# A one-core transformer block: the second batch's attention in two sweeps, with its last projection and routing inside the loop

## What is computed

```
x = x + 0.5 * ffn(layernorm(x))        # first mixture-of-experts layer
x = x + attention(layernorm(x))        # 16 heads, latent width 64, causal
x = x + 0.5 * ffn(layernorm(x))        # second one, same weights
```

```
pos  = cumsum(onehot(expert of each choice)) - 1
keep = pos < 320
out_e = (silu(buf @ wg) * (buf @ wu)) @ wd       # buf: the tokens scattered by (expert, pos)
routed[token] += gate * keep * out_e[expert, pos]
```

## Time and profile before

| | |
|---|---|
| median of 3 runs | 1077.17 us |
| the profiled execution | 1078.49 us, of which its span is 1076.7 us |
| PE busy | 873.8 us, 81% of the span |
| DVE, ACT, POOL busy | 567.6, 406.9, 399.4 us |
| chain that ended last | PE 52%, DVE 15%, POOL 10%, SP queue 7%, DMA 7%, issue 7% |
| mean granted TensorE clock | 0.94 |

### The profile page before, as it was taken

How to read it: one execution, slowest core, us unless ns; L and a number is a source line. 1 busy time by engine, 2 the same in 40 slices (tenths; PEclk the granted TensorE clock), 3 DMA queues, 4 the chain that set the end, 5 groups by cost and what they waited for, 6 DMA issues and landing times.

```text
span 1076.7 us, 16412 instructions
## 1 busy us (share of the span) xinstructions
PE 873.8 (81%) x5041; PEld 720.3 (67%) x5041; DVE 567.6 (53%) x1624; ACT 406.9 (38%) x803; POOL 399.4 (37%) x583
## 2 busy tenths in 40 slices
PE   2358599992678998998999799899999845899993
PEld 1235477771246887987888488888888823687773
DVE  6743245444369665665752575566641362345444
ACT  2101132321314564554641454656566211233323
POOL 2677266654002222221210111354642046356651
PEclk9999699997789999999999899999999868899997
DMA  9510345553620011114101001112110100446536
GB/s 357 205 49 25 104 145 177 172 153 118 196 53 1 20 43 30 43 41 139 30 21 42 1 10 34 42 51 60 47 34 21 40 21 25 146 138 190 167 105 198
DMA packets 96245, 94.11 MB, mean 87 GB/s; under 512 B 15274, under 2 KB 83004, under 8 KB 95415
## 3 DMA queue, kind: packets, MB, share of 16 engines
q1 hardware_dynamic: 86966, 81.00, 25.1%
q0 software_dynamic: 9216, 12.33, 3.7%
HBM read 54.95 MB, written 37.03 MB: 85 GB/s over the span
## 4 chain that ended last, share of the span: by engine, by line
PE 52%; DVE 15%; POOL 10%; SPq 7%; DMA 7%; issue 7%; ACT 1%; POOLq 0%; DVEq 0%; ACTq 0%
PE PS L1375 15%; PE PS L1282 8%; POOL xbuf L552 7%; PE PS L1269 6%; SPq L499 6%; PE PS L1331 5%; PE PS L1270 5%; PE PS L1356 4%; PE PS L1406 3%; DVE mxp L1052 3%; DVE den L1096 2%; DMA rden<-den 2%; DVE xs L1034 2%; PE PS L1243 2%; POOL area_o L588 2%
## 5 line engine op out<-in xcount | busy, mean ns | idle before, releaser
L1375 PE MATMUL PS<-pT,area_v 128*128 128x256 f32 (+1 forms) x1280 | 307.7, 364 | 20.4 <-POOL pT L568 20.2
L1052 DVE TENSOR_REDUCE mxp<-PS 128x2 f32<-128x512 f32 (+1 forms) x320 | 197.7, 630 | 149.5 <-PE PS L1331 81.9
L752 ACT ACTIVATE pT<-PS 128x512 f32<-128x512 f32 (+1 forms) x320 | 176.7, 554 | 186.7 <-PE PS L1356 183.9
L1375 PEld LDWEIGHTS PS<-pT,area_v 128*128 128x128 f32 x1280 | 211.7, 192 | 36.8 <-issue 22.5
L602 POOL DMA_INDIRECT ybuf<-area_o,yidx x160 | 155.6, 973 | 128.5 <-DVE area_o L1008 89.5
L1331 PE MATMUL PS<-Kz,Qx 128*128 128x256 f32 (+1 forms) x640 | 169.0, 355 | 17.5 <-DVE mxp L1052 11.1
L552 POOL DMA_INDIRECT xbuf<-xn,sidx x128 | 125.4, 980 | 88.3 <-issue 62.0
L1356 PE MATMUL PS<-Qx,Kz 128*128 128x256 f32 (+1 forms) x640 | 142.7, 305 | 6.6 <-ACT pT L752 5.5
L1331 PEld LDWEIGHTS PS<-Kz,Qx 128*128 128x128 f32 x640 | 113.6, 196 | 39.0 <-DVE mxp L1052 19.6
L588 POOL TENSOR_TENSOR area_o<-area_o,rden 128x512 f32<-128x512 f32 x32 | 40.7, 1271 | 258.5 <-DMA rden<-den 258.5
L568 POOL TENSOR_SCALAR_AFFINE_SELECT pT<-pT 128x128 f32<-128x128 f32 x256 | 67.7, 299 | 178.9 <-ACT pT L752 178.6
(11 more groups left out here) (160 smaller groups left out, 859.2 us busy)
## 6 DMA issues: line engine op xcount, KB each, us to landing
area_v<-xbuf SPq DMA_DIRECT2D x32, 340.0 KB, 3.2
area_v<-in_L_ffn_wg_dram SPq DMA_DIRECT2D x32, 256.0 KB, 3.4
area_v<-in_L_ffn_wu_dram SPq DMA_DIRECT2D x32, 256.0 KB, 3.7
area_v<-in_L_ffn_wd_dram SPq DMA_DIRECT2D x64, 128.0 KB, 2.5
rden<-den SPq DMA_DIRECT2D x256, 32.0 KB, 1.8
yg<-ybuf SPq DMA_DIRECT2D x24, 256.0 KB, 4.3
qkbuf<-stage SPq DMA_DIRECT2D x24, 256.0 KB, 3.0
xbuf<-Kz SPq DMA_DIRECT2D x4, 1360.0 KB, 10.9
```

The costliest lines, as they stand in the source:

```text
L752: nc.scalar.activation(pT[:, N % 4, 0:w], PS[:, 2 + N % 2, 0:w], ACT.Exp).then_inc(exp_done, 1)
L1052: nc.vector.tensor_reduce(mxp[:, i, c, 2 * hp:2 * hp + 2], PS[:, k % 2, 0:2 * w].rearrange("p (h w) -> p h w", h=2), AX.X, ALU.max).then_i ...
L1375: ins = mm(PS[:, pv_bank(U, a), (p + 1) * TC - w:(p + 1) * TC], value_and_ones(j, h), pT[:, N % 4, a * w:(a + 1) * w], start=(first and p ...
```

## The change

- Steps are numbered over both batches in *visits* (batch, group, chunks). Batch 0 has 4 visits of all four chunks, as before. Batch 1 has 4 visits of chunks 0 to 2 (24 steps each), then 4 visits of chunk 3 (16 steps each), so 12 visits and 12 loads of q and k in place of 8 and 8. A load is 5 DMAs (q of 4 heads in one, k of each head in one; 32 rows a head), not 8. The constant rows of `qkbuf` are written at the start.
- New row items in batch 1's chunk-3 steps: "O" is `out_proj` and residual of one tile (tiles 0 to 5, at steps 272 to 282), "Y" the LN transposes, "S" the scores, "C" the counts of those six tiles. LN statistics, routing (route 4, six tiles) and the Sqrt and Exp tables for them stand between steps 286 and 310; 12 of the 24 scatters of the six tiles stand at steps 313 to 324.
- Tiles 6 and 7 (route 5) follow after the loop, mixed with the shared network (`last_part`). `sil` and `hb` move to the area of the values.
- Row items: 18 ahead of the loop, 186 in batch 0's steps, 169 in batch 1's. Each visit's last T stands right after its last R; before, three items later.
- Start: x arrives as the first DMA, LN and scores of batch 0 are done in halves; one of POOL's two 128x4096 memsets goes behind the first 64 scatters.
- Into attention: combine, LN, J, stores and loads of visit 0 in two halves of 512 tokens; the maxima of chunks 0 and 1 need the first half alone.

Core of the diff (the splitting of `ln`, `shared` and `ln_std_dev` into parts is left out):

```diff
+VISITS = [(0, g, tuple(range(NCH))) for g in range(NG)] + [(1, g, c) for c in (tuple(range(NCH - 1)), (NCH - 1,)) for g in range(NG)]
+STEPS = [(v, c, j, p) for v, (b, g, chunks) in enumerate(VISITS) for c in chunks for j in range(2 * c + 1, -1, -1) for p in range(2)]
+O_STEPS = [FIRST[V_LAST - 2] + 2 * i for i in range(HT - 2)]
+S_STAT, S_ROWS, S_TURN, S_SCORE = FIRST[V_LAST - 1] - 2, FIRST[V_LAST - 1], FIRST[V_LAST - 1] + 1, FIRST[V_LAST] - 1
+S_GROUP, S_EXP, S_HOT, S_GATE, S_COUNT = [FIRST[V_LAST] + k for k in (1, 3, 4, 4, 6)]
+SCAT_LAST = [n for n in range(S_COUNT + 3, len(STEPS) + 5)]
...
+EXTRA = [(O_STEPS[i], ("O", i)) for i in range(HT - 2)] + [(S_TURN, ("Y", 0, 3)), (S_TURN + 1, ("Y", 3, 6)), (S_SCORE, ("S", 4)),
+         (S_COUNT, ("C", 4)), (TAIL, ("O", 6)), (TAIL, ("O", 7)), (TAIL, ("Y", 6, 8)), (TAIL, ("S", 5)), (TAIL, ("C", 5))]
...
+def row_steps():
+    steps, end = [-1] * N_EARLY, 0
+    for v, visit in enumerate(VISITS):
+        mine = [k for k, (vk, item) in enumerate(PLAIN) if vk == v and k >= N_EARLY]
+        last = max(UNIT_FIRST[U] for U, (vu, c) in enumerate(UNITS) if vu == v) - 2
+        begin = 0 if v == 0 else max(end, FIRST[v - 1] + 3)
+        steps += [begin + i * (last - begin) // len(mine) for i in range(len(mine))]
+        end = last
...
-ROUTES = [(0, 0, HT // 2), (0, HT // 2, HT), (1, 0, HT), (0, 0, HT), (1, 0, HT // 2), (1, HT // 2, HT)]
+ROUTES = [(0, 0, HT // 2), (0, HT // 2, HT), (1, 0, HT), (0, 0, HT), (1, 0, HT - 2), (1, HT - 2, HT)]
...
+            def visit_in(v, cols, arrived):
+                b, g, chunks = VISITS[v]
+                heads = qkbuf[b, :, HG * g:HG * g + HG, :, cols]
+                sp.dma_start(Qx[v % 2][:, cols].bitcast(F32), heads[0].rearrange("h r t -> (h r) t")).then_inc(arrived, 16)
                 for hh in range(HG):
+                    sp.dma_start(Kz[v % 2][RW * hh:RW * hh + RW, hh, cols].bitcast(F32), heads[1, hh]).then_inc(arrived, 16)
...
+                if step in FIRST[1:-1]:
+                    v = FIRST.index(step) + 1
+                    sp.wait_ge(st_ready, step)
+                    visit_in(v, slice(0, T), qk_in[v % 2])
-            sp.wait_ge(wo_x, 2 * HT)
+            sp.wait_ge(pv_done, len(STEPS))
             expert_pairs(1)
...
+            def last_part():                     # TensorE
+                pe.wait_ge(exp_done, len(STEPS))
+                pe.wait_ge(y_free, 2 * len(UNITS))
+                gate_up_rows(1, 0)
+                for k in LAST_ROWS[0:2]:
+                    row_item(k)
+                gate_up_rows(1, 1)
+                down_rows(1, 0)
+                for k in LAST_ROWS[2:4]:
+                    row_item(k)
+                gate_up_rows(1, 2)
+                down_rows(1, 1)
+                row_item(LAST_ROWS[4])
+                gate_up_rows(1, 3)
+                down_rows(1, 2)
+                down_rows(1, 3)
...
+            def last_part():                     # VectorE
+                hidden_rows(1, 0)
+                for k in LAST_ROWS[0:2]:
+                    row_item(k)
+                last_stats(1)
+                ln_rows(5, 1, 1, *LN_LAST[1])
+                hidden_rows(1, 1)
+                shared_x(1, 0)
+                for k in LAST_ROWS[2:4]:
+                    row_item(k)
+                for step in (route_groups, route_experts, route_hot):
+                    step(5)
+                hidden_rows(1, 2)
+                shared_x(1, 1)
+                row_item(LAST_ROWS[4])
```

More of the change, by code:

```diff
@@ L60 @@
 RW = 32
-R0 = 2
-RQ = R0 + 3 * HD
+R0 = RW - 3 * HD
 VP = 3 * LAT
@@ L70 @@
 C_TOK, C_EID, C_K, C_N = 560, 576, 581, 585
[L73 to L118, removed]
-def rows_at(step):
-    return [k for k, s in enumerate(ROW_STEP) if s == step]
[L125 to L132, removed]
-LAST = [(0, 1), (1, 3), (3, 6), (6, 8)]
-LAST_PE = 6
-ROUTES = [(0, 0, HT // 2), (0, HT // 2, HT), (1, 0, HT), (0, 0, HT), (1, 0, HT // 2), (1, HT // 2, HT)]
+ROUTES = [(0, 0, HT // 2), (0, HT // 2, HT), (1, 0, HT), (0, 0, HT), (1, 0, HT - 2), (1, HT - 2, HT)]
 L1 = 3
@@ new lines, with rows_at @@
+ROWS = sorted([(step, 0, k, *PLAIN[k]) for k, step in enumerate(row_steps())] +
+              [(step, 1, k, V_LAST, item) for k, (step, item) in enumerate(EXTRA)])
+ROW_STEP = [row[0] for row in ROWS]
+ROW_ITEMS = [row[3:] for row in ROWS]
+ROW_NUMBER = {item if item[0] != "R" else (v, item): k for k, (v, item) in enumerate(ROW_ITEMS)}
+LAST_ROWS = [k for k, step in enumerate(ROW_STEP) if step == TAIL]
+def rows_at(step):
+    return [k for k, s in enumerate(ROW_STEP) if s == step]
+EVAC, RECIP, SCALE_AT, DRAIN = LAG + 1, LAG + 5, LAG + 10, 16
@@ L151, in pv_bank, with units_at @@
+def units_at(step, delay, b):
+    return [U for U, s in enumerate(UNIT_STEP) if s + delay == step and VISITS[UNITS[U][0]][0] == b]
+LAST = [(0, 1), (1, 3), (3, 6), (6, 8)]
+LAST_PE = 6
 def pv_bank(U, a):
@@ L1228, in shared, with down_rows @@
-                down(3)
+                for q in range(4):
+                    gate_up_rows(L, q)
+                    if q:
+                        down_rows(L, q - 1)
+                down_rows(L, 3)
+            def down_rows(L, q):
+                pe.wait_ge(sh_h, 8 * L + 2 * q + 2)
+                if q >= 2:
+                    pe.wait_ge(sh_x, 4 * L + q - 1)
+                for c in range(HC):
+                    for t in range(4):
+                        ins = mm(PS[:, 6 + q % 2, t * D:(t + 1) * D], hb[q % 2][:, c, t * P:(t + 1) * P], sdw[:, c, :],
+                                 start=(c == 0 and t == 0), stop=(c == HC - 1), skip_group_check=True)
+                ins.then_inc(sh_y, 1)
@@ L1413, in _ @@
             pe.wait_ge(s_ctc, 1)
-            ln(0, 0)
-            for f in range(2):
-                scores(f, 0)
+            scores(0, 0)
+            ln_half(0, 0, 1)
+            scores(1, 0)
+            pe.wait_ge(s_cst, 1)
             for f in range(2):
```

693 lines of the change are left out of this document (409 added, 284 removed).

## The result

| | us |
|---|---|
| before, median of 4 runs | 1076.56 (1074.43 to 1077.93) |
| after, median of 4 runs | 1090.56 (1081.44 to 1092.05) |
| ratio | 1.011, interval [1.008, 1.014] |
| forecast | 1049 (1033 to 1064) |

What follows compares the result with a forecast made beforehand. TensorE was taken to bound the attention loops, and chains of waits over other engines the stages between. The terms -5.1 - 27.7 + 1 + 33.5 - 29.8 gave -28.1 us, so 1049 us, range 1033 to 1064.

Steps and rivals of the forecast that it cites:

- Start (-5.1): Before POOL's first scatter: LN and scores in halves save DVE's waits for ACT and scores, 5.1 us, ends 2 and 7.
- Into attention (-27.7): Way to the first attention step: row scores start earlier and fewer items stand ahead of the loop, 27.7 us saved.
- Batch 0's steps (+1): Batch 0's attention loop: three more items and T waits cost, batch 1's combines among fewer items save; 1 us longer.
- The J in group 2 stay as they are: Batch 0's loop: batch 1's q and k projections keep their place, so no cost was added.
- Batch 1's steps (+33.5): Batch 1's attention loop: moved-in row items, O, LN, scores, counts, T waits and loads make it 33.5 us longer.
- The load term, 1.0: Chunk-3 visits of batch 1: waits for q and k loads cost 1.0 us in all, ends 0 and 18.
- The argument against late loads: Chunk-3 sweep: SP has no spreading where loads stand, against the 9% rival of loads waited for in full (1071 us).
- no change, ends -5 and +8: Batch 1's loop: `pv` waits for masks behind `scale` on in-order POOL stay as before, with these ends in us.
- The end (-29.8): Last `pv` to the second expert layer's first transpose: 53.1 us in place of 82.9, with 3.8 for a lower clock.
- The rival of the cold tail: After the loop: TensorE's work stays at 1.2 GHz, some 10 us more, 1059 us; 16%.
- holes filled: Batch 1's loop: new items fall into TensorE's idle time, 14 of 18.6 us go, 1035 us; 14%.
- The rival of a cold sweep: Batch 1's second sweep: waits keep the clock at 1.2 GHz, slower than before; half of it cold gives 1102 us; 4%.

Runs made afterwards that it cites:

- runs 5 and 6: POOL's `scale` put behind later masked steps, in the changed kernel (1056.5 us, ratio 0.980) and in the kernel before (1055.17 us, 0.979).
- run 2: Changed kernel with batch 1's four J in two pairs, at steps 108, 109, 114 and 115: 1081.24 us, ratio 1.002.
- run 1: Changed kernel with the last T of each visit two steps behind its last R: 1082.27 us, ratio 1.005.
- all three edits: Changed kernel with last T two steps later, batch 1's J in two pairs and `scale` behind the masks: 1040.61 us, ratio 0.965.
- run 8: Changed kernel with the T, J and `scale` edits together: 1040.61 us, ratio 0.965 to the kernel before.
- runs 1 to 4: Changed kernel with T moved; J paired; last tiles' items behind the loop; the same with one sweep: 1082.27, 1081.24, 1120.42, 1098.81 us.
- `scale` edit: A unit's `scale` on POOL put behind masked steps of a later unit; in the kernel before: 1055.17 us, ratio 0.979.
- 13 against 11: Two sweeps with T, J and `scale` edits: O of tiles 0 and 1 at the first chunk-3 visit's start (1101.99 us) against without (1109.11).
- Runs 9 to 14: Kernels with the T, J and `scale` edits, in one or two sweeps, some with O early or the tail in halves: ratios 0.960 to 0.968.
- the eleventh run: The two-sweep changed kernel with the T, J and `scale` edits, run again: 1109.11 us, ratio 0.968.

## Why the prediction was wrong

The forecast was -28.1 us for the profiled execution and +13.3 came, a miss of 41.4. Of it 37.0 stands in the two terms of the loops (+1 and +33.5, where +21.4 and +50.1 came): the sum let the waits in TensorE's stream grow by little, and had nothing there for the clock behind them.

- **Start (-5.1): right.** The first scatter at 26.90, 26.7 forecast.
- **Into attention (-27.7): 4.5 us too good.** The J came as forecast. The path from J to the first R took 19.2 us, not 17.1, and 15.5 us followed to the first step, not 13.5: value products of 0.86 to 1.02 us stand between the 14 items (read from the trace, not tested).
- **Batch 0's steps (+1): the failed step, +21.4.** The sum has item counts and T there and no term for masks. Their waits grew from 10.1 to 13.6 us, and with the clock behind them they were worth 10.2 us more than in the kernel before (20.7 against 10.5, runs 5 and 6). "The J in group 2 stay as they are" was wrong: the new list moved them by 11 steps, and TensorE's wait behind SP's spreading grew from 2.45 to 5.46 us, now with the lower clock behind it. Taking the four J apart gave 9.7 us (run 2); how much of it the kernel before would gain too isn't known. T at 0.4 us each summed to 4.8 us in both batches; the trace has 8.1 of waits, and run 1 gave 6 to 7. With all three edits the step is at +1.4, so the count of the items was about right.
- **Batch 1's steps (+33.5): right items, wrong waits, +50.1.** New items 17.6 against 23. The order with its T and loads was priced at 10.5 (6.3 + 3.2 + 1.0) and took 32.5 with the new table (22.8 + 9.7). The load term, 1.0, measured 3.6 in waits and 7.5 with the other waits gone. It had an upper end of 18. The argument against late loads, that SP has no spreading where the loads of this sweep stand, was wrong for the first of them (run 8: issued right behind 22 us of spreading). The masks' "no change, ends -5 and +8" measured +3.9 in waits (10.1 to 14.0), inside its ends. Two errors of opposite sign met: the new items came 5.4 cheaper than priced, which hid a part of the order's 22 us.
- **The end (-29.8): right as a sum,** 54.0 against 53.1, clock dip included: the two O ran at the lower clock (3.78 us for 16 products, 1.98 before), the gate and up products behind them at 1.02, full speed. The parts were later than forecast (`scale` ended at +13.1, not +11.1), and the last eight scatters took 8.9 us from first to last start, not 10. The rival of the cold tail fell with it; "holes filled" fell with the loops. The rest of the span took 159.4 us, 1.0 less than before.
- **What the sum lacked** is a term for the clock. Batch 0: 9.3 us more idle, 12.1 more busy, of which the items were to be 1.0. Batch 1: 16.9 more idle, 33.2 more busy, of which the items were to be 25. So some 11 and 8 us are the same work at a lower clock; the mean clock says the same of batch 0 (0.95 over 261 us is 26 us at half speed, 13 us lost, against 2 before). These are readings of one execution each, and the clock isn't the same in every execution: beside runs 1 to 4 those of the kernel before went from 1072.72 us at a mean clock of 0.943 to 1086.22 at 0.926. I had used for the tail alone. The Trainium skill, "TensorE: Matmul & The Clock Gate", "Why this matters for your kernels", wants the engine free of idle gaps. By that rule the trace agrees in part, even in a loop that is 89% busy: 7 us at 0.63 behind the J gap, and none behind others (last section). The rival of a cold sweep named this mechanism, but only for batch 1's second sweep; it was spread over both batches.
- **What stays open.** With the waits of masks, T and J moved away, the change is worth 14.1 us beside the kernel before with its `scale` edit, and 28.1 was forecast. The missing 14 us are 4.7 on the way into attention and 10.3 in batch 1's steps (the other terms give 1.0 back), where TensorE still waits 7.5 us for loads; that O ahead of such a load gives 7.1 us is shown (13 against 11), the rest isn't taken apart.

## What to carry to other kernels

A loop that keeps TensorE 90% busy is still set by the few waits inside it; before you price items that you put there, list each in-order queue (here POOL's `scale` ahead of masks, SP's spreading ahead of J's stores, ACT's `stage` ahead of exponentials) with what stands right behind each waiting instruction. Price such a wait at its length at least, and give it an upper end for slower work behind it: 24.2 us of such waits were worth 33 in one kernel, 20.2 us were worth 21 in the other. And look at the waits of the kernel before first: the edit that took them away was worth 21 us there by itself, and the whole change with all three edits gave only 14.6 beyond it (1055.17 and 1040.61).

## What the runs showed of the hardware

**A wait of TensorE doesn't always lower its clock.** In the changed kernel, 2.84 us of waiting for masks had slower work behind them, and 2.75 us had none. Both matmuls, then both windows:

```profile
448.45 1.18 PE L1561 MATMUL PS<-pT,area_v 128*128 128x128 f32 x4 [2.84 <-POOL pT L617]
521.13 0.68 PE L1561 MATMUL PS<-pT,area_v 128*128 128x128 f32 x4 [2.75 <-POOL pT L617]
```
```profile
448.40:452.90 4.50, 4.45 (x23) 4.40 (x23) 1.98 (x3) 1.86 (x5) 2.65 (x7) 0.62 0.14 34
521.10:525.60 4.50, 4.47 (x32) 4.29 (x33) 2.64 (x4) 3.18 (x7) 2.62 (x7) 1.00 0.14 35
```

Of the eleven waits of 0.9 us or more in batch 0's steps of the changed kernel, five had a clock of 0.5 to 0.7 in the 4 us behind them (waits of 1.44, 1.77, 2.38, 2.84 and 5.46 us), six had 1.00 (up to 2.75 us). In the kernel before it was one of ten (2.49 us), and waits of 2.33, 2.41 and 2.45 us had 1.00. So the length of the wait alone doesn't tell, and what does isn't known from these runs.

**Runs on one of the chips were longer.** Runs 9 to 14 took some 6% more for every kernel; all of them were on one chip, and none of runs 1 to 8 was. The eighth and the eleventh run are the same kernel, with spans of 1039.0 and 1109.3 us. Of the 70.3 us between them 42.9 lie ahead of the first exponential, above all in one place, DVE's wait ahead of the scores of batch 1's routing at the start (the eighth, then the eleventh):

```profile
DVE yg L987 <- PE PS L1350: 5.0, 1, 5.0
```
```profile
DVE yg L987 <- remote: 28.0, 1, 28.0
```

The rest is spread: 8.9 us in batch 1's steps, 8.7 in the tail, 9.7 behind it. What it is that is late, the profile doesn't name, and no run tells. TensorE's matmuls took the same time within 1% (381 and 384 ns for the most frequent, 275 and 275 for the experts' down products), a scatter 0.98 and 0.97 us, and the mean clock was 0.949 and 0.945.
